# Edge attention on one core: two multiply-and-add merges per window, and node blocks finished in the loop in the last 20 turns only

## What is computed

```python
h_src, h_dst = nfeats[src], nfeats[dst]
e = leaky_relu(concat([h_src, h_dst, efeats]) @ W_attn + b_attn, 0.01)[:, 0]
m = concat([h_src, efeats]) @ W_ne
alpha = exp(e - segment_max(e, dst)[dst]) / segment_sum(exp(e - emax[dst]), dst)[dst]
z = segment_sum(alpha[:, None] * m, dst)
out = layernorm(x + relu(concat([nfeats, z]) @ W_out))
```

## Time and profile before

| | |
|---|---|
| median of 3 runs | 4011.47 us (4008.56 to 4011.75) |
| profiled execution: time, span | 4011.4 us, 4009.5 us |
| busy: VectorE, GpSimd, PE, ScalarE | 3047.5, 2963.8, 2265.5, 2138.1 us |
| TensorE's granted clock, mean | 0.612 of full speed |
| DMA | 630.65 MB, mean 157 GB/s |

### The profile page before, as it was taken

How to read it: one execution, slowest core, us unless ns; L and a number is a source line. 1 busy time by engine, 2 the same in 40 slices (tenths; PEclk the granted TensorE clock), 3 DMA queues, 4 the chain that set the end, 5 groups by cost and what they waited for, 6 DMA issues and landing times.

```text
span 4009.5 us, 52386 instructions
## 1 busy us (share of the span) xinstructions
PE 2265.5 (57%) x10029; PEld 2009.0 (50%) x10030; DVE 3047.5 (76%) x6597; ACT 2138.1 (53%) x3582; POOL 2963.8 (74%) x3133
## 2 busy tenths in 40 slices
PE   1665665455555555555555555555555555555555
PEld 1555555455555555554555555555455554555554
DVE  8777776777777777777777777777777777777776
ACT  2665555455555555555555555555555555555554
POOL 7777777777777777777777777777777777777770
PEclk9666665656556556566665666555655666556665
DMA  7665555555555555555555555555555555555552
GB/s 164 180 173 160 158 158 158 141 154 160 158 158 159 160 160 160 158 160 157 157 159 157 159 159 160 160 160 158 159 158 157 159 159 156 159 160 160 160 159 83
DMA packets 420774, 630.65 MB, mean 157 GB/s; under 512 B 219681, under 2 KB 220065, under 8 KB 420600
## 3 DMA queue, kind: packets, MB, share of 16 engines
q1 hardware_dynamic: 307240, 521.72, 42.0%
q0 software_dynamic: 100000, 102.60, 14.6%
q10 hardware_dynamic: 13360, 4.87, 0.7%
HBM read 621.58 MB, written 7.07 MB: 157 GB/s over the span
## 4 chain that ended last, share of the span: by engine, by line
DVE 48%; issue 23%; POOL 13%; DVEq 8%; PE 4%; ACT 3%; DMA 0%; ACTq 0%; POOLq 0%
POOL V L424 13%; DVE um L887 10%; DVE prod L673 9%; DVE u L678 9%; DVE psS L750 4%; PE psG L1049 3%; DVE acc L756 3%; DVE acc L761 2%; DVE bounds L890 2%; DVEq L940 2%; DVE nn L892 1%; DVE picked L879 1%; DVE e L745 1%; DVEq L867 1%; ACT L568 1%
## 5 line engine op out<-in xcount | busy, mean ns | idle before, releaser
L424 POOL DMA_INDIRECT V<-in_x_dram,srcs x3125 | 2962.9, 948 | 955.1 <-issue 948.8
L1049 PE MATMUL psG<-V,pT 128*128 128x130 f32 x6250 | 1458.5, 426 | 478.4 <-DVE psS L750 478.4
L1049 PEld LDWEIGHTS psG<-V,pT 128*128 128x128 f32 x6250 | 1357.8, 329 | 612.1 <-DVE psS L750 612.1
L1042 PE MATMUL psT<-ident,e 128*128 128x128 f32 x3125 | 682.2, 387 | 1162.8 <-DVE e L745 1161.6
L1042 PEld LDWEIGHTS psT<-ident,e 128*128 128x128 f32 x3125 | 543.0, 212 | 1264.2 <-DVE e L745 1262.8
L500 ACT COPY pT<-psT 128x512 f32<-128x512 f32 x784 | 420.5, 589 | 1246.4 <-PE psT L1042 1242.8
L745 DVE TENSOR_TENSOR e<-zb,psE 128x1024 f32<-128x1024 f32 x392 | 478.7, 1221 | 381.9 <-issue 206.0
L673 DVE TENSOR_TENSOR prod<-V,psM 128x512 f32<-128x512 f32 x782 | 502.3, 684 | 90.3 <-DMA V<-in_x_dram,srcs 71.7
L887 DVE CUSTOM_DVE_ANT_0 um<-ubc,psS 128x1024 f32<-128x1024 f32 x391 | 477.5, 1221 | 96.6 <-ACT psS L517 95.7
L678 DVE TENSOR_REDUCE u<-prod 128x8 f32<-128x1024 f32 x391 | 477.0, 1220 | 13.5
L535 ACT ACTIVATE psE<-um,ebias 128x1024 f32<-128x1024 f32 x391 | 438.0, 1120 | 12.7
(11 more groups left out here) (137 smaller groups left out, 1036.8 us busy)
## 6 DMA issues: line engine op xcount, KB each, us to landing
ubc<-scores SPq DMA_DIRECT2D x391, 512.0 KB
dbc<-in_dst_dram SPq DMA_DIRECT2D x390, 512.0 KB, 4.3
V<-in_edge_attr_dram SPq DMA_DIRECT2D x390, 256.0 KB, 3.0
V<-in_x_dram,srcs POOLq DMA_INDIRECT x3125
srcs<-in_src_dram SPq DMA_DIRECT2D x390, 4.0 KB
scores<-u SPq DMA_DIRECT2D x390, 4.0 KB
out_dram<-ro SPq DMA_DIRECT2D x159, 32.0 KB
xt<-in_x_dram ACTq DMA_DIRECT2D x6, 448.0 KB, 13.9
```

Of the source, the lines that this page charges most:

```text
L424: nc.gpsimd.indirect_dma_start(Vx[:, s, j, 1:XW], None, x[:, :], bass.IndirectOffsetOnAxis(ap=srcs[:, s, j:j + 1], axis=0)).then_inc(h_in[ ...
L1042: last = nc.tensor.transpose(psT[:, i, (j - 4 * i) * P:(j - 4 * i + 1) * P], e1[:, 0:n * P].rearrange("q (p j) -> q j p", j=n)[:, j, :], i ...
L1049: last = nc.tensor.matmul(psG[:, 0:AW], pT[:, i, (j - 4 * i) * P:(j - 4 * i + 1) * P], V[:, LEADIN + s * SLOT + XW * j:LEADIN + s * SLOT + ...
```

## The change

share_out and merge are replaced by merge_both: two scalar_tensor_tensor operations, one a block. Each reads psG, multiplies by the half's mark as a per-node scalar, adds the accumulator's block and writes it there. The first increments `added`, the second `merged`; rescale waits for both. The scratch in psS is no longer written.

YT, the first turn with finishing, is split. YT = 7 stays where the y steps end; EV = TURNS - ceil(NB / 5) = 39 - 20 = 19 is the first turn with events, and EVENTS is 100. VectorE, PE and ScalarE have one loop more, turns 7 to 18, without finishing; tabulate() moves behind it, and all counts of events start from EV.

```diff
-    EVENTS = (TURNS - YT) * RING // 2
+    EV = TURNS + (-NB // (RING // 2))
+    EVENTS = (TURNS - EV) * RING // 2
...
-            def share_out(tb):
+            def merge(tb, bb, k):
+
+                b = bass.ds(bb + k, 1)
+                return nc.vector.scalar_tensor_tensor(accv[:, b, :].rearrange("p b f -> p (b f)"), psG[:, 0:AW], half[:, bass.ds(tb, 1), k],
+                                                      accv[:, b, :].rearrange("p b f -> p (b f)"), ALU.mult, ALU.add)
+
+            def merge_both(tb, bb):
 
                 dve.wait_ge(turned, g)
-                nc.vector.tensor_tensor(shares, psG[:, 0:AW].unsqueeze(1).broadcast_to((P, 2, AW)),
-                                        half[:, bass.ds(tb, 1), :].rearrange("p a k -> p (a k)").unsqueeze(2).broadcast_to((P, 2, AW)), ALU.mult).then_inc(merged, 1)
-
-            def merge(bb):
-
+                merge(tb, bb, 0).then_inc(added, 1)
+                merge(tb, bb, 1).then_inc(merged, 1)
+
+            def rescale(bb):
+
+                dve.wait_ge(added, g)
                 dve.wait_ge(merged, g)
-                nc.vector.tensor_tensor(accv[:, bass.ds(bb, 2), :], accv[:, bass.ds(bb, 2), :], shares, ALU.add).then_inc(added, 1)
...
+            with dve.Fori(YT, EV) as k:
+                counts(k)
+                for s in range(RING):
+                    supertile(k, s, RING, PAIRS + 1 if s == 0 else None)
             tabulate()
-            with dve.Fori(YT, TURNS - 1) as k:
+            with dve.Fori(EV, TURNS - 1) as k:
                 counts(k, finish)
                 for s in range(RING):
-                    supertile(k, s, RING, PAIRS + 1 if s == 0 else None, True)
+                    supertile(k, s, RING, None, True)
...
+            with pe.Fori(YT, EV) as k:
+                counts(k)
+                for s in range(RING):
+                    supertile(RING * k + s, s, True)
+            with pe.Fori(EV, TURNS) as k:
                 counts(k)
                 for s in range(RING):
                     if s % 2:
                         z_step(k, s // 2)
                     supertile(RING * k + s, s, True)
```

More of the change, by code:

```diff
@@ L67, in graph_attention @@
     assert TURNS * RING == NT - 1 and JL * P + (NT - 1) * ST == E and 4 < JL < J
-    assert E >= ST and 4 < BACK <= 8 and 0 < LAST and TURNS > YT + 2
+    assert E >= ST and 4 < BACK <= 8 and 0 < LAST and TURNS > EV + 2 and EV > YT + 1
     assert YT * YS == PAIRS and 2 * PAIRS == NB and YS <= RING and YT < TURNS - 1
@@ L360, in store_rows @@
                 sp.dma_start(out[bass.ds(at * P, P), :], ro[:, q, :]).then_inc(rows_out[q], 16)
-            with sp.Fori(1, YT + 2) as k:
+            with sp.Fori(1, EV + 2) as k:
                 for s in range(RING):
@@ L365, in _ @@
             sp.wait_ge(table, 1)
-            with sp.Fori(YT + 2, TURNS - 1) as k:
+            with sp.Fori(EV + 2, TURNS - 1) as k:
                 finished(k)
@@ L403, in _ @@
             for q in range(GROUP):
-                sp.wait_ge(rows_out[q], 16 * (TURNS - YT) + (32 if q < GROUP - 1 else 16))
+                sp.wait_ge(rows_out[q], 16 * (TURNS - EV) + (32 if q < GROUP - 1 else 16))
             sp.wait_ge(back_rows, 1)
@@ L568, in deviations @@
                 nc.scalar.activation(junk[:, :], epsv[:, :], ACT.Exp)
-            act.wait_ge(table, 1)
-            with act.Fori(YT, TURNS) as k:
+            with act.Fori(YT, EV) as k:
+                counts(k)
+                for s in range(RING):
+                    supertile(k, s, True)
+            with act.Fori(EV, TURNS) as k:
                 counts(k)
@@ L852, in tabulate @@
                 step(nc.vector.memset(order[:, :], 0.0))
[L853 removed]
+                step(nc.vector.tensor_scalar(reach[:, :], firsts[:, RING * EV:RING * EV + 2 * EVENTS:2], float(NB - 3), None, ALU.min))
                 step(nc.vector.tensor_tensor_scan(final[:, :], ones[:, :], reach[:, :], 0.0, ALU.add, ALU.min))
                 for j in range(GROUP + 2):
[L856 removed]
+                    step(nc.vector.tensor_copy(turns[:, EV:TURNS, 2 * RING + j], order[:, j:j + EVENTS:GROUP]))
                 step(nc.vector.tensor_copy(ends_f[:, 1:2], turns[:, TURNS, 0:1]))
@@ L895, in supertile @@
                                                    ALU.add, ALU.min).then_inc(node_set, 1)
-                    share_out(tb)
-                    merge(bb)
+                    merge_both(tb, bb)
                     rescale(bb1)
@@ L973, in _ @@
             dve.wait_ge(alpha_done, g)
-            share_out(tb)
-            merge(bb)
+            merge_both(tb, bb)
             rescale(bb1)
+            dve.wait_ge(rescaled, g)
             pass_on()
             b, tb, bb, bb1 = offsets()
-            share_out(tb)
-            merge(bb)
+            merge_both(tb, bb)
             dve.wait_ge(added, g)
+            dve.wait_ge(merged, g)
             dve.sem_inc(all_merged, 1)
@@ L1108, in _ @@
             y_multiply().then_inc(y_ready, 1)
-            pe.wait_ge(table, 1)
-            with pe.Fori(YT, TURNS) as k:
+            with pe.Fori(YT, EV) as k:
+                counts(k)
+                for s in range(RING):
+                    supertile(RING * k + s, s, True)
+            with pe.Fori(EV, TURNS) as k:
                 counts(k)
@@ L1116, in _ @@
             late = pe.alloc_register("late_pe")
+            pe.wait_ge(table, 1)
             pe.load(coming[0:1], ends[0:1, 1:2])
```

35 lines of the change are left out of this document (16 added, 19 removed).

## The result

| | before | changed |
|---|---|---|
| median | 4011.57 us (4008.56 to 4011.75, 4 runs) | 3982.22 us (3977.91 to 3985.03, 4 runs) |
| profiled execution: time, span | 4011.4, 4009.5 us | 3981.76, 3979.9 us |
| ratio | | 0.9928 (95% interval 0.9910 to 0.9945) |

The change makes the kernel 0.7% faster, 29.4 us. The forecast was 3975.6 us with a range of 3966 to 3990: the bound, the direction and most of the gain are right, 6.6 us of the forecast gain did not come.

What follows compares the result with a forecast made beforehand. GpSimd's gathers, 100.2 us a turn, stand behind a VectorE 38 us late. Last product at 3924.9 plus 48.8 gives a span of 3973.7; with 1.9 above it 3975.6 us, 0.9% faster, range 3966 to 3990.

Steps and rivals of the forecast that it cites:

- GpSimd needs 100.2 us for a turn, whatever VectorE does: GpSimd's gathers: 1.252 us each, 10 supertiles of 8 a turn, a pace the change does not touch.
- 38 us of lag: End of the kernel: last product 40.65 us behind the last gather against 2.6 when keeping up; the difference can be won.
- the table's 10.3 us: VectorE's table of finished blocks: its turn took 111.40 us instead of 101.08; one term in the lag's sum of 41.1.
- 0.14 us: VectorE, rescale behind the second merge: a dependent operation starts 0.14 us after the one before, as L756 to L761.
- 0.38 us saved per window: VectorE, merge to rescale: 0.78 us instead of 1.16, which is 3.8 us a turn; bounds 0.15 and 0.50.
- The estimate of 260 ns a merge and 396 + 331 ns for the pair removed: Skill page's table for PSUM-sourced VectorE operations, as a cross-check: saving 0.2 us plus the wait gone.
- 3.0 us each: that covers it: PE's 390 waits for L745 ahead of its transposes hide that `merged` comes 0.20 us later; uncovered, 78 us.
- The tail: Last product to the end of the span: 49.2 us before, 48.8 forecast, with 0.38 saved by the merge of supertile 389.
- GpSimd's pace: Rival: the gathers' own pace changes; 1% on 1.252 us is 39 us and would undo the gain; chance 0.02.
- The merge saves nothing: Rival: second merge waits out the first, only the twelve turns count, 10.9 us, 4000.6 us; chance 0.06 (half ways included).
- The start of the turn grows: Rival: VectorE's 6 us stall at finishing turns' starts grows; 4042 us if doubled; 0.04 slower, 0.03 gain only eaten.

Runs made afterwards that it cites:

- seven-gather runs: Kernel before and changed kernel, each without the eighth gather of every supertile from turn 1 on: 3963.65 and 3733.59 us, one run each.
- the merge alone: Changed kernel with the old EVENTS and loops put back, so only the new merge and finishing from turn 7: 3987.37 us, ratio to before 0.9938.
- late finishing alone: Changed kernel with the old share_out and merge put back, so only finishing from turn 19 instead of 7: 3996.76 us, ratio to before 0.9962.
- the one-tensor rescale alone: Changed kernel with the rescale in two steps reading one SBUF tensor each in all turns, merges not moved: 3990.06 us, ratio to before 0.9942.
- the two versions with the one-tensor rescale: Changed kernel with that rescale in all turns, with the merges ahead of the node update (3967.99 us) or where they were (3990.06 us).
- the best one: Changed kernel with the merges ahead of the node update and the one-tensor rescale in all turns: 3967.99 us, ratio to before 0.9889.

## Why the prediction was right, and where it was off

**The bound.** "GpSimd needs 100.2 us for a turn, whatever VectorE does" is the sentence that carried the forecast. For its first half the seven-gather runs speak: with one gather in eight left out the change is worth 230 us. Its second half was wrong, see below.

**The lag.** That 38 us of lag are all there is to win, and go when a finishing turn of VectorE gets shorter than GpSimd's, held: 5.6 us were left in the changed kernel, 6.2 with the merge alone. Where VectorE's turn stayed 0.4 to 0.7 us longer than GpSimd's, with late finishing alone and with the one-tensor rescale alone, 17.8 and 24.4 us were left. In the sum of the lag the table's 10.3 us are too small: turn 6, which it lengthened to 111.40 us, was not yet a finishing turn, and against GpSimd's 100.2 it is 11.2.

**The merge.** 356 ns were forecast, 348 came; the second merge overlapped the first (0.61 us for the two), and the register instructions ahead of it cost nothing. The step that was too small is the wait behind it: 0.14 us taken from a pair of long operations, 0.22 measured. "0.38 us saved per window" is 0.28. The estimate of 260 ns a merge and 396 + 331 ns for the pair removed was off as well: a merge took 348 ns and either of the pair 0.43 us, and L756 reads psS as L750 reads psG, so the two should have had the same figure.

**PE's cover.** "3.0 us each: that covers it" failed in part. The extra wait for ScalarE's squares, 0.8 us a turn, comes with the merge, and the prediction put nothing at that place; a VectorE that stands there sooner explains it as well as a later `merged`. Another 0.4 us a turn, ahead of the end of the z step, have a cause that stays open. A finishing turn is 99.0 us, not 97.3, and the slack 1.2 us, not 2.9. The table's 10 us took the turns to 25 to work off (the lag was 9.1 us at supertile 200 and 3.7 at 250), not four. Nothing of it reached the time, and that was luck in part: any slack is enough for this sum, and with half as much saved there would have been next to none.

**The tail.** 48.8 us forecast, 50.0 measured: the merge of supertile 389 saves nothing, probably since PE is behind it, and the fold of the last supertile's block now waits for a store:

```profile
3938.34 0.15 DVE L793 TENSOR_SCALAR fl<-acc 128x1 f32 x1 [0.59 <-DVE acc L766]
...
3957.89 0.22 DVE L813 TENSOR_REDUCE fm<-fout 128x1 f32<-128x64 f32 x1 [1.11 <-DMA out_dram<-ro]
```

The first idled 0.24 to 0.25 us in the other windows; the second waited 0.34 us in the kernel before. In all the stretch is 0.8 us longer than before (49.2 us), where it was forecast to be 0.36 shorter.

**GpSimd's pace.** The miss of 4.7 us. The forecast gave a change of pace 2 in 100, because the mean was the same beside a less and a more loaded VectorE. It is not the load that counts but the kind of operand, and where it falls. In the finishing turns of the changed kernel 53 gathers of 1195 are long, between 2300 and 3800 us; in the kernel before 36 of 1198. The rescale makes the difference: 41 of the 53 begin beside it, with 7.1 us of excess, and 25 of the 36, with 2.8 us; finishing work accounts for 12 and 11. Over the whole execution the excess is 18.7 us against 14.4, 4.3 of the 4.7. Why gathers start inside the rescale more often and earlier in the changed kernel is not shown: the rescale itself is the same instruction, and VectorE is now in step with the gathers.

**The rivals.** "The merge saves nothing" fell: 4000.6 us was its time, and late finishing alone gave 3996.8. "The start of the turn grows" fell: 89.1 us in fifteen turns are 5.9 each, as before, and the plain turns have 2.4. But it can happen: in the two versions with the one-tensor rescale the plain turns begin with 5.1 us (55.8 us in eleven turns of the best one), and only their slack hides it.

## What to carry to other kernels

Two engines with busy shares of 76% and 74% can both be a bound: compare their time per turn of the loop in one stretch, and look at how far the one has fallen behind the other at the end. An improvement on the slower one is worth at most that lag, however much time it takes off; taking one unit of work from the other engine shows at once what lies behind it. When an engine that issues gathers is the bound, look at which operands its neighbour reads while a gather begins.

## What the runs showed of the hardware

A gather that begins while VectorE is in an operation with two SBUF tensors, or in the faster form with one, is longer by what is left of that operation less 0.12 to 0.13 us (135 lengthened gathers in three kernels); one that begins in its first 0.03 to 0.04 us is not, and lengthens the operation. Some 165 us of two-tensor operations cost GpSimd 20 us. With the second operand in PSUM, at the same duration (480 and 554 ns against 485 and 564), the extra is at most 0.01 us (126 gathers), and the operation takes the same time in every case (553 to 556 ns on 384 columns; with two SBUF tensors 557 to 608).

A gather issued by GpSimd took 1.2485 us from start to start in some executions and 1.2508 in others, 7 us over 3125 of them.

A scalar_tensor_tensor of 130 columns from PSUM with a scalar from memory takes 348 ns, and two without a wait between them 0.61 us together.
